# Start-up order, zero fills, weight preparation, expert registers and row-call spacing in a routed transformer kernel

## What is computed

```python
x = x + 0.5 * moe(layernorm(x))      # 8 experts, top 2 of 8, 128 -> 512 -> 128, relu
x = x + attention(layernorm(x))      # 16 heads of 8, rotary, causal
x = x + 0.5 * moe(layernorm(x))
x = x + 0.5 * quantised_linear(layernorm(x))
x = x + gated_scan_and_ffn(layernorm(x))
x = x + 0.5 * quantised_linear(layernorm(x))
# moe: h = relu(z @ W1[e] + b1[e]); y = h @ W2[e] + b2[e], summed with the two gates
```

## Time and profile before

| | us |
|---|---|
| median of 3 runs (lowest, highest) | 975.32 (974.37, 977.39) |
| the profiled execution | 978.61 |
| its span, first to last instruction | 976.8 |
| PE, DVE, ACT, POOL busy | 837.3, 623.6, 550.1, 666.3 |
| mean granted PE clock | 0.949 |

### The profile page before, as it was taken

One profiled execution on the slowest core, in us unless ns is written; L12 is line 12 of the kernel. 1 busy time (PEld: TensorE's weight loads), 2 busy tenths in 40 slices (PEclk: granted clock), 3 DMA queues, 4 the chain that ended last, 5 costly groups with the idle time before them and its releaser, 6 DMA issues.

```text
span 976.8 us, 23169 instructions
## 1 busy us (share of the span) xinstructions
PE 837.3 (86%) x7489; PEld 615.0 (63%) x7489; DVE 623.6 (64%) x1918; ACT 550.1 (56%) x1221; POOL 666.3 (68%) x851
## 2 busy tenths in 40 slices
PE   2279568987999999999999999999997998757884
PEld 2279568963856576564557555668975997434553
DVE  7650016267589687789978977884435346597674
ACT  2234234436576767666766767677663556744751
POOL 6728996788894337888741897884599983786342
PEclk9999869998999999999999999999998999776897
DMA  8958446583844343453444353433532771110000
GB/s 316 331 209 237 126 130 182 172 225 105 232 141 120 98 136 111 139 157 97 136 116 134 89 152 111 127 92 99 170 111 90 218 219 41 35 28 33 1 11 32
DMA packets 117271, 129.65 MB, mean 133 GB/s; under 512 B 14883, under 2 KB 84643, under 8 KB 117030
## 3 DMA queue, kind: packets, MB, share of 16 engines
q1 hardware_dynamic: 108966, 111.39, 38.8%
q0 software_dynamic: 8192, 16.79, 5.9%
HBM read 87.37 MB, written 40.37 MB: 131 GB/s over the span
## 4 chain that ended last, share of the span: by engine, by line
PE 36%; POOL 34%; DVE 12%; issue 8%; ACT 6%; DMA 3%; SPq 1%; POOLq 0%; DVEq 0%; ACTq 0%
PE bank L765 32%; POOL small L1642 10%; POOL z_scratch L1651 8%; POOL yg L1664 7%; PE bank L777 4%; POOL P L1686 4%; DVE sm_m L1277 2%; DMA yg<-y_scratch,pos 2%; POOL sm_f L1621 1%; ACT P L1441 1%; ACT P L1523 1%; DVE xs L1215 1%; POOL ab L1674 1%; DMA z_scratch<-P 1%; DVE xs L1218 1%
## 5 line engine op out<-in xcount | busy, mean ns | idle before, releaser
L1277 DVE TENSOR_REDUCE sm_m<-bank 128x4 f32<-128x512 f32 (+2 forms) x320 | 204.8, 682 | 52.3 <-PE bank L765 49.6
L1523 ACT ACTIVATE P<-bank 128x512 f32<-128x512 f32 x320 | 173.8, 596 | 32.9 <-PE bank L765 27.3
L765 PE MATMUL bank<-w2r,hb 128*128 x1360 | 188.5, 283 | 0.0
L765 PE MATMUL bank<-zt,wt 128*128 128x128 f32 x1360 | 181.5, 284 | 4.3 <-ACT zt L1466 3.4
L1686 POOL TENSOR_SCALAR_AFFINE_SELECT P<-P 128x256 f32<-128x256 f32 (+1 forms) x320 | 116.1, 383 | 96.4 <-ACT P L1523 92.6
L765 PEld LDWEIGHTS bank<-zt,wt 128*128 128x128 f32 x1360 | 166.6, 197 | 13.4 <-issue 4.8
L1651 POOL DMA_INDIRECT z_scratch<-zb,pos x128 | 131.6, 1028 | 59.5 <-issue 24.6
L765 PEld LDWEIGHTS bank<-w2r,hb 128*128 128x128 f32 x1360 | 166.2, 193 | 2.6 <-issue 0.7
L1482 ACT ACTIVATE hb<-bank 128x512 f32<-128x512 f32 x170 | 100.9, 596 | 96.2 <-PE bank L765 83.3
L1642 POOL TENSOR_TENSOR small<-small 128x4 f32<-128x4 f32 x137 | 145.4, 1061 | 10.6 <-DVE pos L1201 7.2
L1664 POOL DMA_INDIRECT yg<-y_scratch,pos x128 | 130.6, 1020 | 23.7 <-issue 20.7
(11 more groups left out here) (219 smaller groups left out, 1407.6 us busy)
## 6 DMA issues: line engine op xcount, KB each, us to landing
wt<-w_scratch SPq DMA_DIRECT2D x170, 256.0 KB
zin<-z_scratch SPq DMA_DIRECT2D x82, 128.0 KB
y_scratch<-yt SPq DMA_DIRECT2D x82, 128.0 KB
q_scratch<-qpart SPq DMA_DIRECT2D x48, 128.0 KB
k_scratch<-kpart SPq DMA_DIRECT2D x48, 128.0 KB
Ks<-k_scratch SPq DMA_DIRECT2D x64, 96.0 KB
Qs<-q_scratch SPq DMA_DIRECT2D x64, 96.0 KB
z_scratch<-P SPq DMA_DIRECT2D x6, 512.0 KB, 5.7
```

The lines of the kernel that those rows point to most:

```text
L765: return e.matmul(o, lhs, rhs, start=start, stop=stop, **kw)
L1277: e.tensor_reduce(to, of, AX.X, ALU.max, negate=True).then_inc(*d_max.step(i, f"m{s_}"))
L1523: e.activation(P[:, (2 * i + s_) % PR, :], shared("scor", i, 0, s_), ACT.Exp, scale=SCALE).then_inc(*a_sc.step(i, f"e{s_}"))
```

## The change

- The start DMAs become a planned stage `begin` of six steps, both first batches of x ahead of the constants; the fills become stages `zero` (FIRST_FILL) and `fill` (LATER_FILL), planned straight behind it, and `scat` of phases 0 and 1 is planned behind them.
- `wr` is no longer loaded (eight DMAs of 256 KB). `split` is one PE matmul with a 128x128 matrix `less` (a new DMA of 64 KB) and one ACT copy for each expert, planned behind the PE step of the first `route`. b1 is written to `w_scratch` by one more DMA, which SP waits for before the first `wload`.
- ACT runs one small Exp ahead of everything.
- `route`: two multiplies and two reduces become one of each; `ei` is a planned step of its own, so that the wait of the plan for the combine of phase f-2 stands only there. In `bias`, the second step is planned behind the first `route`.
- SP and PE read the experts of up to four blocks by one load.
- Spacing: ROWS_CLOSE (1.35 us) is planned for `scat` of phase 0 and `comb` of the last phase, where `pause` then never applies; ROWS_APART elsewhere.

The diff, cut to its core:

```diff
-LATER_FILL = pieces_of(0, PHASE[0].blocks * SB, SLOTS) + pieces_of(1, 0, SLOTS)
+LATER_FILL = pieces_of(1, 0, SLOTS) + pieces_of(0, PHASE[0].blocks * SB, SLOTS)
...
-    "sload": ("S0.95+6",
+    "begin": ("S0.9+2.6 S0.47+2.6<-1 S1.9+2.4<-1 S1.9+2.7<-1 S0.47+2.3<-1 S0.02+0.0<-1",
+    "sload": ("S0.47+4.5",
-    "split": ("G1.25 S0.52+4",
+    "split": ("P0.97+0.2 A0.6+0.15 S0.52+4",
+            [(0, 1)], 1),
+    "zero": ("S1.4+8",
+    "fill": ("S2.4+10",
-    "route": ("P0.2+0.2 D4.9+0.15",
+    "route": ("P0.2+0.2 D3.3+0.15 D1.1+0.15",
-    "wload": ("S1.1+4.5",
+    "wload": ("S0.75+4.5",
...
-ROWS_APART, ROWS_CALL = 2.2, 1.15
+ROWS_CLOSE, ROWS_APART, ROWS_CALL = 1.35, 2.2, 1.15
...
-        return [("sload", u, 0)] if k == 0 else []
+        return [("sload", u, 0), ("route", 0, 0)] if k == 0 else []
...
-        return [("route", OF_TILE[u], 1)] if k == 0 else []
+        return [("route", OF_TILE[u], 1)] + ([(("zero", "fill")[OF_TILE[u]], 0, 0)] if OF_TILE[u] < 2 else []) if k == 0 else []
...
-def moves_rows(stage, u, k):
+def moves_rows(stage, k):
-    return k < 2 and (stage == "scat" and OF_TILE[u] > 0 or stage == "comb")
+    return k < 2 and stage in ("scat", "comb")
+def apart(stage, u):
+    return ROWS_CLOSE if (stage, OF_TILE[u]) in (("scat", 0), ("comb", PHASES - 1)) else ROWS_APART
...
-                if between + ROWS_CALL < ROWS_APART - 0.25:
+                if between + ROWS_CALL < apart(stage, u) - 0.25:
...
+        def experts(e, f, k, row):
+            n = min(4, PHASE[f].blocks - k)
+            _, found = nc.values_load_multi_w_load_instructions(ei[0:1, f % 2, k:k + n], engines=(e.engine,), min_val=0,
+                                                                max_val=128 * (NE - 1))
+            row.update({PHASE[f].block + k + i: at for i, at in enumerate(found)})
...
             def sload(n):
                 e.dma_start(P[:, n, :], a["w1"][n]).then_inc(l_raw[n], 16)
-                e.dma_start(last_row(n), a["wr"][n]).then_inc(l_raw[n], 16)
-                if n == NE - 1:
-                    fill(FIRST_FILL, l_zero0)
+                yield
+            def first_fill(_):
+                fill(FIRST_FILL, l_zero0)
                 yield
...
-                if n == 5:
-                    fill(LATER_FILL, l_zero)
...
                 if u == 0:
                     w.wait_ge(s_w, 16 * NE)
+                    e.dma_start(wd.rearrange("(e r) c -> e r c", r=128)[:, D - 1, :], a["b1"]).then_inc(l_b1, 16)
+                    w.wait_ge(l_b1, 16)
...
-                row = e.value_load(ei[0:1, f % 2, k:k + 1], min_val=0, max_val=128 * (NE - 1))
-                e.dma_start(wt[u % WR][:, :], wd[bass.DynSlice(row, 128), :]).then_inc(l_wt[u % WR], 16)
+                if k % 4 == 0:
+                    experts(e, f, k, row)
+                e.dma_start(wt[u % WR][:, :], wd[bass.DynSlice(row.pop(u), 128), :]).then_inc(l_wt[u % WR], 16)
...
+            def split(n):
+                w.wait_ge(l_less, 16)
+                w.wait_ge(l_raw[n], 16)
+                o = take("split", n, 0, a_split.at(n, "w"))
+                mm(o, less_last, P[:, n, :], True, True).then_inc(*t_split.step(n, "w"))
...
-                for k, oh in ((1, o1), (2, o2)):
-                    then(e.tensor_tensor(by_j(m_), oh[:, 0:T, :], by_j(ps), ALU.mult), f"m{k}")
-                    then(e.tensor_reduce(pf[:, k - 1, :], by_j(m_), AX.X, ALU.add), f"p{k}")
+                then(e.tensor_tensor(m_, oh[:, :, 0:T, :], by_j(ps).unsqueeze(1).to_broadcast([128, 2, T, 8]), ALU.mult), "m")
+                then(e.tensor_reduce(pf, m_, AX.X, ALU.add), "p2")
...
+            w.wait_ge(*d_init.at(0, "half"))
+            e.activation(early, mhalf, ACT.Exp)
...
-                e.tensor_tensor(P[:, n, :], P[:, n, :], last_row(n), ALU.subtract).then_inc(*p_split.step(n, "w"))
```

More of the change, by code:

```diff
@@ L184, in follows @@
 def follows(stage, u, k):
-    if stage in ("first", "sload"):
+    if stage == "begin":
         return []
+    if stage == "first":
+        return [("begin", 0, 2 + k)]
+    if stage == "sload":
+        return [("begin", 0, 5)]
+    if stage == "wquant":
+        return [("begin", 0, 3)] if k == 0 else []
     if stage == "xload":
-        return [("sload", NE - 1, 0)]
+        return [("begin", 0, 5)]
+    if stage in ("zero", "fill"):
+        return [("begin", 0, 5)]
     if stage == "late":
-        return [("xload", NB - 3, 0), ("split", NE - 1, 1)]
+        return [("xload", NB - 3, 0), ("split", NE - 1, 2)]
     if stage == "split":
-        return [("sload", u, 0)] if k == 0 else []
+        return [("sload", u, 0), ("route", 0, 0)] if k == 0 else []
     if stage == "prep":
         if k == 0:
-            return [("prep", u - 2, 9), ("heads", USES[u][1], 3) if USES[u][0] == 2 else ("xload", USES[u][1] - 2, 0)]
+            return [("prep", u - 2, 9), ("heads", USES[u][1], 3) if USES[u][0] == 2 else ("xload", USES[u][1] - 2, 0) if USES[u][1] >= 2 else ("begin", 0, USES[u][1])]
         if k == 3:
@@ L214, in follows @@
     if stage == "bias":
-        return [("first", 0, 1)] if k == 0 else []
+        return [[("first", 0, 1), ("begin", 0, 4)], [("route", 0, 1)], [], []][k]
     if stage == "res":
@@ L254, in network @@
 def network():
-    counts = {"first": 1, "xload": NB - 2, "late": 1, "sload": NE, "split": NE, "wquant": 1, "prep": 2 * NB, "route": PHASES, "scat": NTILE,
+    counts = {"begin": 1, "first": 1, "xload": NB - 2, "zero": 1, "fill": 1, "late": 1, "sload": NE, "split": NE, "wquant": 1, "prep": 2 * NB, "route": PHASES, "scat": NTILE,
               "bias": 1,
@@ L346, in forward @@
         free[engine] = start + steps[k][1]
-        if moves_rows(stage, u, k):
-            free["R"] = start + ROWS_APART
+        if moves_rows(stage, k):
+            free["R"] = start + apart(stage, u)
         done[stage, u, k] = free[engine] + steps[k][2]
@@ L385, in backward @@
         free[key[2]] = left[x] = end + plan[x[0]][0][x[2]][1]
-        if moves_rows(*x):
-            free["R"] = end + ROWS_APART
+        if moves_rows(x[0], x[2]):
+            free["R"] = end + apart(x[0], x[1])
         del known[key]
@@ L498, in build @@
         tri, ones = sb("tri", [128, 128], BF16), sb("ones", [128, 128], BF16)
-        small = sb("small", [128, SMALL + 22])
-        spare = small[:, SMALL + 18:SMALL + 22]
+        small = sb("small", [128, SMALL + 26])
+        spare, early = small[:, SMALL + 18:SMALL + 22], small[:, SMALL + 22:SMALL + 26]
         kth, iota = small[:, 0:KB], small[:, 80:88]
@@ L548, in build @@
         t_route = flow("t_route", "n")
-        d_route = flow("d_route", "t i c n e s b b2 p m1 p1 m2 p2 pos k k2 ei")
+        d_route = flow("d_route", "t i c n e s b b2 p m p2 pos k k2 ei")
         t_zin, a_zin = flow("t_zin", "z"), flow("a_zin", "z")
@@ L752, in mxb @@
                 yield
-            begin()
-            follow("S", {"sload": sload, "split": split, "xload": xload, "late": late, "wload": wload, "zin": zin, "res": res, "proj": proj, "stack": stack,
+            follow("S", {"begin": begin, "sload": sload, "split": split, "xload": xload, "zero": first_fill, "fill": later_fill, "late": late, "wload": wload, "zin": zin, "res": res, "proj": proj, "stack": stack,
                          "mrow": mrow, "mxb": mxb})
@@ L824, in hid @@
                 w.wait_ge(*d_route.at(f, "ei"))
-                row[u] = e.value_load(ei[0:1, f % 2, k:k + 1], min_val=0, max_val=128 * (NE - 1))
+                if k % 4 == 0:
+                    experts(e, f, k, row)
                 yield
@@ L1047, in gated @@
                 yield
-            follow("P", {"prep": prep, "route": route, "zin": zin, "hid": hid, "res": res, "proj": proj,
+            follow("P", {"prep": prep, "split": split, "route": route, "zin": zin, "hid": hid, "res": res, "proj": proj,
                          "maxi": maxi, "mrow": mrow, "scor": scor, "val": val, "heads": heads, "wquant": wquant,
@@ L1169, in route @@
                 by_e = lambda ap: ap.rearrange("p (e j) -> p e j", e=8)[:, :, 0:T]
-                tot, inc, base, ps, m_ = (rt[:, i, :] for i in range(5))
+                tot, inc, base, ps = (rt[:, i, :] for i in range(4))
+                m_ = rt[:, 4:6, 0:8 * T].rearrange("p a (j e) -> p a j e", e=8)
                 n_, ends, start, fl = rs[:, 0:8], rs[:, 8:16], rs[:, 16:24], rs[:, 24:24 + KB]
@@ L1459, in prep, with split @@
                 yield
+            def split(n):
+                w.wait_ge(*t_split.at(n, "w"))
+                e.activation(P[:, n, :], shared("split", n, 0), ACT.Copy).then_inc(*a_split.step(n, "w"))
+                yield
             def zin(n):
```

61 lines of the change are left out of this document (37 added, 24 removed), and 2 rows, old and new, of the table STAGES.

## The result

The changed kernel takes **962.88 us** (median of 4 runs, 961.48 to 964.75) where the kernel before takes 975.88 beside it: ratio 0.9868, 95% interval 0.9842 to 0.9894. That is 13.0 us, of a forecast of 21.8 (953.5 us, 942 to 968). It lies inside that range, and outside the narrower 945 to 961 to which the forecast itself gave 0.51. The profiled execution took 964.75 us with a span of 963.0, 13.8 less than the span before.

What follows compares the result with a forecast made beforehand. PE was taken to bound 200 to 800 us, POOL's late scatter calls the hole before, order and latency the tail. Front 16.6 (11.3 + 5.3) plus spacing 5.2 gave 21.8 us off 975.3: 953.5 us, range 942 to 968.

Steps and rivals of the forecast that it cites:

- Fills ahead: Zero fills issued early, so the first scatter call of phase 1 no longer waits for them: 11.3 us gained there.
- The bound of 1.2 us for the traffic: Upper bound for some 0.5 MB more DMA traffic at the start if all were on the path; taken as 0.
- The start: Chain up to the first scatter call of phase 0, shortened by five edits on ACT, DVE and POOL: together 5.3 us.
- W1 on PE and ACT: New matmuls and copies beside the 16 scatter calls, 8.2 to 16.3 us on PE; 8.2 on the path if uncovered.
- SP's wait for the stores and the b1 row: Wait ahead of the first weight loads, late constants and zins: taken as 0, 6.5 us if the cover is gone.
- POOL still decides, and all 16.6 us pass on: First scatter call of phase 1 comes 16.6 us earlier, and POOL, not PE's phase 0 ending at 107.0, sets phase 1.
- The forecast 117.6: Predicted time of the first expert matmul of phase 1 on PE, 134.21 before, 16.6 us earlier.
- Registers ... I take 0: Merged register loads for up to four blocks: no gain taken, bounds 0 and PE's 26.7 us idle from 200 to 800.
- Spacing: Five pauses of 1.05 us go from the last phase's gathers: 5.2 us gained, bounds 0 and 16.3.
- The first, 964.0: Rival: only the fills' wait is gained, units 2 to 4 do not move with the start, DVE binds the tail; chance 0.20.
- The middle did not stall: Rival: new order stalls PE from 200 to 800 us, idle above 26.7 of 600 us, 998.8 us; chance 0.06.
- The close calls did not lengthen: Rival: all 24 last gathers lengthen to the longest seen, 0.70 us above the median, 16.7 us, 970.2 us; chance 0.05.

## Why the prediction was right or wrong

**Fills ahead (forecast 11.3): right in the mechanism.** In the old kernel it is worth 11.5 us by the ratio. That this meets the forecast so closely is in part luck, since the first call moved only 9.2 us and phase 1 on PE 7.4. The bound of 1.2 us for the traffic was about right in the changed kernel (1.1 to 2.4 at the start of phase 0). In the old one, with `wr` still loaded, phase 0 starts 4 us later.

**The start (forecast 5.3): right up to the first call.** The first call of phase 0 came 5.0 earlier. The small DVE steps that took 0.90 and 1.00 us beside POOL's subtractions take 0.17:

```profile
0.79 1.28 ACT L1666 ACT_TABLE_LOAD   x1 [0.79 <-PEq L1877]
...
14.76 0.17 DVE L1188 TENSOR_TENSOR sm_p<-sm_p 128x4 f32<-128x4 f32 x1
...
16.02 0.17 DVE L1200 TENSOR_SCALAR gate<-gate 128x4 f32<-128x4 f32 x1
```

W1 on PE and ACT was covered by the scatter calls, as forecast. SP's wait for the stores and the b1 row was not free: it holds the late constants until they crowd the landing of phase 0's rows, so that phase 0 starts 1.5 us earlier and not 5.3. What the start is worth at the end is a remainder, with an uncertainty of about 5 us: the change with single loads has 19.7 us, the fills and close gathers in the old kernel 13.9, which leaves 5.8 for the start and all other parts. No run held the start alone. By the page ScalarE: Activation LUTs of the Trainium skill (section "What ACT_TABLE_LOAD costs") the estimate was 1.4 us more; the trace has 1.28 us for the load, now at 0.79, and nothing here shows a drain on top: the next ACT instruction starts at 2.09.

**"POOL still decides, and all 16.6 us pass on": wrong in the reason, nearly right in size.** The scatter calls came 19.4 earlier rather than 16.6, by the earlier preparation of units 2 to 4. But PE's phase 0 moved 1.5 us and not 5.3: ahead of it PE waits 7.61 us for a `zb` and 1.21 for `zin`, both behind the late landing. So PE ended phase 0 near 110, not 107.0, and it took over from POOL, through the router logits behind phase 0: the experts of phase 1 came 15.5 earlier. The forecast 117.6 was met within 1.1 us by another path. How much of the front reaches the end depends on the order of taking it. By the fills in the old kernel and the remainder it is 11.5 + 5.8 = 17.3 us; by what the changed kernel keeps with spaced gathers (2.7) and regains with single loads (6.8) it is 9.5.

The granted clock is no part of this. Its column has 0.50 (1.2 GHz, the lower of two levels) from 35 to 60 us where it had 1.00 before, but four transposes of one shape take the same time in both, and about half where PE is in full flow. Two rows of before, then two of after:

```profile
41.42 1.11 PE L777 MATMUL bank<-ident,zb 128*128 128x128 f32 x4
109.95 0.60 PE L777 MATMUL bank<-ident,zb 128*128 128x128 f32 x4
...
26.82 0.60 PE L815 MATMUL bank<-ident,zb 128*128 128x128 f32 x4
40.94 1.11 PE L815 MATMUL bank<-ident,zb 128*128 128x128 f32 x4 [2.66 <-ACT zb L1488]
```

So by its matmuls the kernel before ran this stretch at the lower rate too, whatever its column says.

**"Registers ... I take 0": the term that was mis-sized most clearly.** The merged loads cost 5 us by the medians and 7 by the ratios (0.9868 against 0.9798). The forecast had it between 0 and a gain of 26.7, and left out a loss; the old trace showed that single loads are hidden behind a full PE, which says nothing of a load and eight register instructions in a row. With this term at -5 to -7, the forecast 21.8 becomes 15 to 17.

**Spacing (forecast 5.2): half of it in the old plan, twice in the new.** The edit brings 2.7 us when added to the old kernel, and costs 10 when taken from the new. Five pauses of 1.05 us were not its price: in the wide plan of the changed kernel five pauses cost 1.1 us together, and in the close one ten cost 9.8. The other part of the edit, a spacing that the planner works with, was costed at nothing, and it decides what stands between the gathers. The 10 us are no sum of terms: with spaced gathers the new plan loses what it won in front, while the old plan does not. Why the new order is the more sensitive one stays open.

A sum in one order of taking it is 11.5 (fills) + 2.7 (gathers, together measured as 13.9) + 5.8 (start and the rest) - 6.8 (loads of four) = 13.2, against 12.9 measured. It proves nothing by itself, since the 5.8 is the remainder that makes it close. In this kernel the gathers give more than their forecast and the loads of four take it back: the errors offset each other in part, and that is luck.

**Rivals.** The first, 964.0, names nearly the measured time, but not by its mechanism: the preparation of units 2 to 4 did move with the start, and an unforeseen cost took as much back. The middle did not stall, PE idle 29.6 of 600 us. The close calls did not lengthen: median 979 ns with a longest of 1477, against 1012 and 1708. By the rule in SBUF — State Buffer ("SBUF: two separate sides") of the Trainium skill they should have, where DVE's work beside them is two-port. Which of it is, the profile does not say; in this stretch no such effect shows.

**A version that beats both** is the change with single register loads on PE (958.08 us), or on both engines (957.89): 1.8 to 2.1% below the kernel before, and 5 us below the change.

## What to carry to other kernels

When an instruction is hidden behind a full engine, cost its replacement by the longest run of it that stands in one place, not by how many there are in all. A wait at the front that a whole phase stands behind can be worth most of its length even in a kernel whose bound is elsewhere. Ask where each transfer goes that is put off: here the late constants, held back 6 us by a longer wait, fell on the landing of the rows that the next phase waits for. A spacing or a cost handed to a planner is an edit to the order of everything around it: test the number and the instruction that enforces it apart from each other.

## What the runs showed of the hardware that was not expected

- One load of four registers on PE with its eight register instructions cuts PE's stream for 0.53 us per four blocks; four loads of one register each leave the stream whole at 4.01 us for two blocks. On SP the same replacement changes nothing in the time (957.89 against 958.08).
- The column of the granted clock can be wrong for a stretch. From 35 to 60 us the kernel before shows 1.00, yet four 128x128 fp32 transposes take 1.11 us there, as in the changed kernel at 0.50, and 0.60 us at 109.95. A matmul form that recurs is a check of the column.
- The rows of the last scatter call land about 2.4 us behind its start when the DMA engines have room (51.99 to 54.36 before; 48.19 to 50.71 with the constants ahead) and 5.8 us when they are full (47.79 to 53.59 in the changed kernel; up to 7.3 in the others with this start).
- In the changed start two scatter calls lengthen:

```profile
27.52 1.57 POOL L1700 DMA_INDIRECT z_scratch<-zb,pos  x1 [0.20 <-issue]
...
30.66 2.12 POOL L1700 DMA_INDIRECT z_scratch<-zb,pos  x1 [0.30 <-issue]
```

With the second fill late the second of these is back at 0.98 us (30.48) and the first is not (1.57 at 27.35). What lengthens them was not tried.
